# One input of four for a state-space scan computed on GpSimd instead of on VectorE, with its operands in SBUF

## What is computed

```
h = exp(dt_t[..., None] * A) * h + (dt_t * u_t)[..., None] * B_t[:, :, None, :]
y = jnp.einsum('bkdn,bkn->bkd', h, C_t)
```

## Time and profile before

| | |
|---|---|
| median of 3 runs | 13,516.15 us (13,488.19 to 13,520.65) |
| the profiled execution, its own time | 13,515.58 us |
| its span, first to last instruction | 13,513.4 us |
| VectorE busy | 11,024.0 us, 82% |
| TensorE matmul busy | 9,861.3 us, 73% |
| GpSimd busy | 8,026.4 us, 59% |
| ScalarE busy | 7,165.5 us, 53% |
| granted TensorE clock, mean | 0.701 of full speed |

### The profile page before, as it was taken

One profiled execution on the slowest core, in us unless ns is written; L12 is line 12 of the kernel. 1 busy time (PEld: TensorE's weight loads), 2 busy tenths in 40 slices (PEclk: granted clock), 3 DMA queues, 4 the chain that ended last, 5 costly groups with the idle time before them and its releaser, 6 DMA issues.

```text
span 13513.4 us, 97205 instructions
## 1 busy us (share of the span) xinstructions
PE 9861.3 (73%) x27968; PEld 2433.4 (18%) x27968; DVE 11024.0 (82%) x6747; ACT 7165.5 (53%) x10802; POOL 8026.4 (59%) x3463
## 2 busy tenths in 40 slices
PE   6866677766886677768777778776688667777665
PEld 1211112111221112212222112211122111221121
DVE  2999977998799988988789887899878998898700
ACT  3645545544465445666456654555446554576324
POOL 1667655666566766666666665566656776666500
PEclk8955577755786568769777777865679557776565
DMA  2655576555745555455564557655675555554410
GB/s 71 132 118 112 108 135 112 127 115 109 140 119 115 116 140 132 107 120 118 143 124 108 117 120 134 112 118 109 120 131 128 117 115 138 121 120 108 99 51 14
DMA packets 1742497, 1551.92 MB, mean 115 GB/s; under 512 B 1302398, under 2 KB 1303712, under 8 KB 1741964
## 3 DMA queue, kind: packets, MB, share of 16 engines
q1 hardware_dynamic: 1741964, 1545.71, 53.9%
HBM read 555.57 MB, written 184.55 MB: 55 GB/s over the span
## 4 chain that ended last, share of the span: by engine, by line
PE 27%; issue 26%; DVE 23%; ACT 8%; DMA 7%; POOL 4%; SPq 4%; DVEq 1%; POOLq 0%; ACTq 0%
DVE ps L1228 15%; DVE hs L1237 7%; PE ps L644 4%; PE ps L796 4%; DMA ust<-u_d 3%; PE ps L783 3%; PE ps L758 3%; PE ps L617 3%; POOL pr L1305 3%; PE ps L774 2%; ACT dec L1024 2%; PE ps L661 1%; DMA sd<-y_d 1%; SPq L528 1%; POOL sd L1273 1%
## 5 line engine op out<-in xcount | busy, mean ns | idle before, releaser
L1305 POOL TENSOR_TENSOR pr<-hs,crep 128x1024 f32<-128x1024 f32 x3072 | 7223.0, 2353 | 4490.9 <-DVE hs L1237 3209.6
L1237 DVE TENSOR_TENSOR_SCAN hs<-dec,carry,ps 128x1024 f32<-128x1024 f32 x2304 | 5406.4, 2347 | 303.6 <-ACT dec L1024 9.6
L1228 DVE TENSOR_TENSOR ps<-ps,dur 128x1024 f32<-128x1024 f32 x3072 | 3722.2, 1212 | 1038.3 <-PE ps L783 833.7
L783 PE MATMUL ps<-sbc,selb 96*128 96x512 bf16 x6144 | 2553.4, 510 | 2195.5 <-DVE hs L1237 2182.7
L1024 ACT ACTIVATE dec<-dtr,ac 128x1024 f32<-128x1024 f32 x3072 | 3489.8, 1137 | 981.8 <-DVE hs L1237 971.5
L796 PE MATMUL ps<-pr,red 128*32 128x512 f32 x12288 | 2387.8, 861 | 12.6 <-ACT yst L1039 7.0
L1031 ACT ACTIVATE carry<-hs 128x1 f32<-128x1 f32 x2304 | 460.2, 200 | 2758.7 <-DVE hs L1237 2755.7
L1237 DVE TENSOR_TENSOR_SCAN hs<-dec,zero,ps 128x1024 f32<-128x1024 f32 x768 | 1802.3, 2347 | 100.8 <-ACT dec L1024 2.9
L783 PEld LDWEIGHTS ps<-sbc,selb 96*128 96x128 bf16 x6144 | 510.0, 110 | 5057.2 <-DVE hs L1237 3847.0
L617 PE MATMUL ps<-xb,tapw 96*96 96x512 f32 x2304 | 1204.6, 635 | 21.0 <-ACT sd L871 18.5
L774 PE MATMUL ps<-xdf,tapw 6*96 6x512 f32 x1024 | 812.6, 884 | 166.1 <-ACT sbc L997 113.8
(11 more groups left out here) (113 smaller groups left out, 6108.7 us busy)
## 6 DMA issues: line engine op xcount, KB each, us to landing
dtr<-de SPq DMA_DIRECT2D x768, 512.0 KB, 7.6
dur<-us SPq DMA_DIRECT2D x768, 512.0 KB, 8.5
crep<-c_d SPq DMA_DIRECT2D x512, 512.0 KB, 6.9
ust<-u_d SPq DMA_DIRECT2D x256, 384.0 KB, 7.5
y_d<-yst SPq DMA_DIRECT2D x768, 128.0 KB, 3.7
sd<-y_d SPq DMA_DIRECT2D x512, 192.0 KB, 4.2
u_d<-sd SPq DMA_DIRECT2D x64, 384.0 KB, 3.1
z_d<-sd SPq DMA_DIRECT2D x64, 384.0 KB, 4.2
```

The costliest lines, as they stand in the source:

```text
L783: mm = pe.matmul(ps[:, SLOT + 2 * (n % RS) + hf, :], selb[:, i % GT // 2, :], sbc[:, w % 2, B * hf:B * (hf + 1)], start=True, stop=True)
L1228: dve.tensor_tensor(slot(n), slot(n), dur[:, 2 * (G % 2) + i % 2, :], ALU.mult).then_inc(bu_v, 1)
L1237: dve.tensor_tensor_scan(hs[:, n % RH, :], dec[:, n % RD, :], slot(n), init, ALU.mult, ALU.add).then_inc(scan_v, 1)
L1305: pool.tensor_tensor(pr[:, n % RP, :], hs[:, n % RH, :], crep[:, q, :], ALU.mult).then_inc(prod_g, 1)
```

## The change

For tiles 6 and 7 of each group (`on_pool`) TensorE makes no fill and VectorE no multiply. B of the last 4 states is spread by a DMA into a new SBUF buffer `brep`, and GpSimd multiplies `dur` by it in place. The scan of such a tile reads its decays and its input from SBUF. The other six tiles keep the PSUM path, and are renumbered by `others(n)` and `other(m)`, so that their slots, semaphore counts and look-ahead run over them alone: while tiles 6 and 7 are under way, the slots of the next group's first tiles can be filled.

With it go these: B is stored beside C (`bc_d`, 128 KB instead of 64 KB) and `load_b` is issued at tile 1; `load_u` is issued at tile 6 of step w for step w+2, where that belongs to the same sequence; `load_group` waits for the scans of the group whose room it takes, not for its multiplies; `yst` has one buffer instead of two, which makes room for `brep`.

```diff
+def on_pool(n):
+    return n % GT >= GT - 2
+def others(n):
+    return (GT - 2) * (n // GT) + min(n % GT, GT - 2)
+def other(m):
+    return GT * (m // (GT - 2)) + m % (GT - 2)
...
+            def load_b(w):
+                after(sp, bup_g, 2 * NG * w)
+                sp.wait_ge(c_out, 16 * (w + 1))
+                sp.dma_start(brep[:, :], bc_d[w % 2, NS - 4:NS, :].partition_broadcast(DB)).then_inc(brep_in, 16)
...
-                after(sp, bu_v, GT * (G - 1))
+                after(sp, scan_v, GT * (G - 1))
...
                     if i == 1:
+                        load_b(w)
                         load_c(NQ - 1, w)
-                        if w + 1 < W:
+                        if w + 1 < W and (w == 0 or (w + 1) % STEPS == 0):
                             load_u(w + 1)
+                    if i == 6 and w + 2 < W and (w + 2) % STEPS:
+                        load_u(w + 2)
...
-                after(pe, scan_v, n - RS + 1)
+                m = others(n)
+                after(pe, scan_v, other(m - RS) + 1 if m >= RS else 0)
...
-                    if n + 1 < W * NT:
-                        fill(n + 1)
+                    if not on_pool(n) and others(n) + 1 < W * NT * (GT - 2) // GT:
+                        fill(other(others(n) + 1))
...
-                after(act, y_out[E % 2], 32 * (E // 2))
+                after(act, y_out, 32 * E)
...
+                if on_pool(n):
+                    G = n // GT
+                    dve.wait_ge(bup_g, 2 * G + i % 2 + 1)
+                    dve.tensor_tensor_scan(hs[:, n % RH, :], dec[:, n % RD, :], dur[:, 2 * (G % 2) + i % 2, :], init,
+                                           ALU.mult, ALU.add).then_inc(scan_v, 1)
...
                 for i in range(NT):
-                    inp(w * NT + i)
+                    if not on_pool(i):
+                        inp(w * NT + i)
...
+            def input_on_pool(n):
+                w, G, j = n // NT, n // GT, n % 2
+                pool.wait_ge(bu_v, others(n - 2) + 1)
+                if n % NT == GT - 2:
+                    pool.wait_ge(brep_in, 16 * (w + 1))
+                v = dur[:, 2 * (G % 2) + j, :]
+                pool.tensor_tensor(v, v, brep[:, :], ALU.mult).then_inc(bup_g, 1)
...
                     product(w * NT + i)
+                    if i % GT in (3, 4):
+                        input_on_pool(w * NT + i + 3)
```

More of the change, by code:

```diff
@@ L141, in build_program @@
     t_d = dram("t_d", [nb, 2, CH, L])
-    c_d = dram("c_d", [2, NS, T])
+    bc_d = dram("bc_d", [2, 2 * NS, T])
     ctx = ExitStack()
@@ L168, in build_program @@
         crep = sb("crep", [128, NQ, T])
-        yst = sb("yst", [128, 2, B])
+        yst = sb("yst", [128, B])
+        brep = sb("brep", [128, T])
         carry = sb("carry", [128, NT])
@@ L284, in build_program @@
         ye_a = sem("ye_a")
-        y_out = [sem("y_out0"), sem("y_out1")]
+        y_out = sem("y_out")
+        brep_in, bup_g = sem("brep_in"), sem("bup_g")
         x_in = sem("x_in")
@@ L426, in post @@
                 cnt = done["post"]
-                for r in range(2):
-                    sp.wait_ge(y_out[r], 32 * (NG * STEPS // 2) * (j + 1))
+                sp.wait_ge(y_out, 32 * NG * STEPS * (j + 1))
                 after(sp, uz_out, 32 * C8 * done["pre"])
@@ L507, in store_c @@
                 sp.wait_ge(xd_a, 2 * w + 2)
-                sp.dma_start(c_d[w % 2], xdf[NS:2 * NS, :]).then_inc(c_out, 16)
+                sp.dma_start(bc_d[w % 2], xdf[0:2 * NS, :]).then_inc(c_out, 16)
             def load_c(q, w):
@@ L512, in load_c @@
                 sp.wait_ge(c_out, 16 * (w + 1))
-                sp.dma_start(crep[:, q, :], c_d[w % 2, 4 * q:4 * q + 4, :].partition_broadcast(DB)).then_inc(crep_in[q], 16)
+                sp.dma_start(crep[:, q, :], bc_d[w % 2, NS + 4 * q:NS + 4 * q + 4, :].partition_broadcast(DB)).then_inc(crep_in[q], 16)
+            def load_b(w):
+                after(sp, bup_g, 2 * NG * w)
+                sp.wait_ge(c_out, 16 * (w + 1))
+                sp.dma_start(brep[:, :], bc_d[w % 2, NS - 4:NS, :].partition_broadcast(DB)).then_inc(brep_in, 16)
             def load_group(g, w):
@@ L536, in store_y @@
                     sp.dma_start(y_d[s, k][2 * DB * g:2 * DB * (g + 1), t0:t0 + B],
-                                 yst[64 * hf:64 * (hf + 1), E % 2, :]).then_inc(y_out[E % 2], 16)
+                                 yst[64 * hf:64 * (hf + 1), :]).then_inc(y_out, 16)
             run(beside(plan[0], stages, False))
@@ L780, in fill @@
                     pe.wait_ge(s_a, 6 * w + 6)
-                after(pe, scan_v, n - RS + 1)
+                m = others(n)
+                after(pe, scan_v, other(m - RS) + 1 if m >= RS else 0)
                 for hf in range(2):
-                    mm = pe.matmul(ps[:, SLOT + 2 * (n % RS) + hf, :], selb[:, i % GT // 2, :],
+                    mm = pe.matmul(ps[:, SLOT + 2 * (m % RS) + hf, :], selb[:, i % GT // 2, :],
                                    sbc[:, w % 2, B * hf:B * (hf + 1)], start=True, stop=True)
@@ L995, in split @@
                 else:
-                    after(act, fill_p, NT * (w - 1))
+                    after(act, fill_p, others(NT * (w - 1)))
                 act.activation(sbc[:, w % 2, B * hf:B * (hf + 1)], ps[0:CH, PB, :], ACT.Identity).then_inc(s_a, 1)
@@ L1036, in collect @@
                 act.wait_ge(red_p, NP * w + NQ * (g + 1))
-                after(act, y_out[E % 2], 32 * (E // 2))
-                for dst, src in to_image(order[s][1], k, yst[:, E % 2, :], ps[:, YB, :]):
+                after(act, y_out, 32 * E)
+                for dst, src in to_image(order[s][1], k, yst[:, :], ps[:, YB, :]):
                     ins = act.activation(dst, src, ACT.Identity)
@@ L1226, in inp @@
                     dve.wait_ge(du_in[G % 2], 32 * (G // 2 + 1))
-                dve.wait_ge(fill_p, n + 1)
-                dve.tensor_tensor(slot(n), slot(n), dur[:, 2 * (G % 2) + i % 2, :], ALU.mult).then_inc(bu_v, 1)
+                dve.wait_ge(fill_p, others(n) + 1)
+                dve.tensor_tensor(slot(others(n)), slot(others(n)), dur[:, 2 * (G % 2) + i % 2, :], ALU.mult).then_inc(bu_v, 1)
             def states(n):
@@ L1234, in states @@
                 after(dve, carry_a, carries(n - RH + 1) if n >= RH else 0)
-                dve.wait_ge(bu_v, n + 1)
                 init = carry[:, i:i + 1] if w % NCH else zero[:, 0:1]
-                dve.tensor_tensor_scan(hs[:, n % RH, :], dec[:, n % RD, :], slot(n), init, ALU.mult, ALU.add).then_inc(scan_v, 1)
+                if on_pool(n):
[3 more added lines that the diff above has]
+                                           ALU.mult, ALU.add).then_inc(scan_v, 1)
+                else:
+                    dve.wait_ge(bu_v, others(n) + 1)
+                    dve.tensor_tensor_scan(hs[:, n % RH, :], dec[:, n % RD, :], slot(others(n)), init,
+                                           ALU.mult, ALU.add).then_inc(scan_v, 1)
             run(beside(plan[0], stages, False))
```

## The result

The changed kernel takes 14,045.85 us (median of 4 runs, 14,031.88 to 14,062.75) against 13,508.3 us of the kernel before, measured beside it: a ratio of 1.040, 95% interval 1.0381 to 1.0419. That is 538 us slower. The forecast was 13,815 us, in a range of 13,340 to 14,060: the sign and the mechanism were right, the size was not, since 300 us were forecast.

The account below looks back on a forecast made before the run. VectorE's chain was taken as the bound, 11,060 us plus some 1,455 of lateness from side work. The sum was 13,515.6 + 909 - 400 - 100 - 190 + 80 = 13,815 us, range 13,340 to 14,060.

Parts of the forecast that it names:

- The exclusion: A VectorE instruction with two SBUF inputs and a GpSimd instruction reading SBUF wait for each other; scans near 4.5 us.
- The quiet group: Eight tiles with hardly any side work: 1.7 us longer, the third group 3.7; a step 93.5 us, +909 us in all.
- the recovery: What takes up part of the 909 us: fill waits, early load, late groups, against dearer side work in `post`.
- (a): VectorE's waits for fills, 833.7 us, fall by missing fills and look-ahead: -400 us, bounds -208 and -650.
- (b): `load_u` issued a step earlier removes ScalarE's and TensorE's waits for it: -100 us, bounds 0 and -206.
- (c): Where a stall falls in tiles 4 or 5, scan 6 isn't held: 90 groups, -190 us, bounds 0 and -400.
- (d): GpSimd's multiply in `post` queues behind new inputs and blocked products while TensorE waits: +80 us, bound +290.
- Kept ports: Rival, chance 0.18: VectorE runs scans 6 and 7 in succession before product 5; a step 89.3 us, total 13,390 us.
- no exclusion for long scans: Rival, chance 0.06: long scans and GpSimd don't block each other; a step 78.4 us, total 12,500 to 12,700 us.
- waits merely change places: Rival, chance 0.03: either this or a larger recovery pays back the cost; total 13,516 us within 0.3%.
- GpSimd as the bound in `post`: Rival, chance 0.06: GpSimd also limits the steps with `post`, little is recovered and `load_b` is late; up to 14,506 us.
- costed at nothing: `load_b`, `load_c`, `dur` loads, one `yst` buffer and the larger store were expected to delay nothing; `load_b` uncovered would be +250 us.

Follow-up runs that it names:

- the two experiments above: Kernel before, VectorE's multiply of tiles 6 and 7 writing to SBUF: 14,242.19 us; changed kernel, decays of tiles 6 and 7 in PSUM, fill look-ahead dropped: 13,095.2 us.
- the late load: The changed kernel with the u values of step w+1 loaded at tile 1 of step w again: 14,314.35 us, ratio 1.0605.
- the last experiment: GpSimd's side work put ahead of each tile's product and input: changed kernel 14,040.09 us, with decays in PSUM 13,085.21, kernel before 13,510.48.

## Why the prediction was right, and what was mis-sized

**The exclusion** held, in both directions. The trace of before had shown it only on instructions of 1 and 96 elements, and it holds for scans of 1024. The Trainium skill (SBUF — State Buffer, § Who interferes with whom) states the rule for two-input instructions as such; the two experiments above, 3,334 ns with both inputs in SBUF and 2,326 with one in PSUM, agree.

**The quiet group** was sized right: 93.5 us for a step was forecast, 93.0 measured, and scans on `dur` near 4.5 us were 4,536 and 4,450 ns. First scans of two steps in a row, with no stall between them, in the kernel before and in the changed one:

```profile
1084.82 2.35 DVE L1237 TENSOR_TENSOR_SCAN hs<-dec,carry,ps 128x1024 f32<-128x1024 f32 x1
...
1171.32 2.35 DVE L1237 TENSOR_TENSOR_SCAN hs<-dec,carry,ps 128x1024 f32<-128x1024 f32 x1
```

```profile
4566.52 2.35 DVE L1269 TENSOR_TENSOR_SCAN hs<-dec,carry,ps 128x1024 f32<-128x1024 f32 x1
...
4659.46 2.35 DVE L1269 TENSOR_TENSOR_SCAN hs<-dec,zero,ps 128x1024 f32<-128x1024 f32 x1
```

A step went from 86.50 to 92.94 us, 6.44 more. Of 909 us on paper 128 x 6.44 = 824 came. In the third group the order was not the one worked out: scan 6 was to run right after product 4, and input 7 and product 5 went ahead of it. The two scans still ended 13.2 us after the start of scan 5, as forecast, because the same operations stand in a row in either order. That part of the size was right by this, not by the order.

**The step that failed is the recovery**, terms (a) to (d), -610 us. It came to 524 (the difference of the spans) - 824 = -300.

(b), forecast -100: the early load is worth -268 in the changed kernel, outside the bounds of 0 to -206. They were taken from its wait in the kernel before, and the change itself would have tripled that wait.

So (a), (c) and (d) together brought about -300 + 268 = -32 instead of -510 (the -268 is a difference between rounds, with its 15 us of doubt). VectorE's largest waits in the changed kernel:

```profile
DVE ps L1254 <- PE ps L809: 522.8, 219, 19.6
DVE sd L1186 <- ACT ps L929: 316.7, 50, 36.0
DVE xb L1191 <- PE ps L686: 262.5, 61, 7.8
```

(a): waits for fills fell by 311 us, from 833.7. But with the late load they are 706.1, so the change's own part, missing fills and look-ahead, is 128 us of it. Taken from the other side, with the early load in both kernels, it is 677.8 - 522.8 = 155. 400 had been forecast, and 208 was the low bound.

(c): all holds come to 1,640 us. VectorE's timeline in a quiet step gives this for the two scans together, of the first, the second and the third group:

```profile
4586.80 8.69 DVE L1265 TENSOR_TENSOR_SCAN hs<-dec,carry,dur 128x1024 f32<-128x1024 f32 x2
...
4617.03 8.69 DVE L1265 TENSOR_TENSOR_SCAN hs<-dec,carry,dur 128x1024 f32<-128x1024 f32 x2
...
4647.26 10.94 DVE L1265 TENSOR_TENSOR_SCAN hs<-dec,carry,dur 128x1024 f32<-128x1024 f32 x2
```

Unheld they would take 2.26 + 2.35 = 4.61. A quiet step holds its scans 2 x 4.08 + 6.33 = 14.5 us. That would be 1,855 us in 128 steps, so in all they were held about 215 us less. The trace bears the mechanism out: in 99 of the 384 groups the scan of tile 4 or 5 starts over 0.8 us late, and these groups are held 153 us less in all than the groups of the same place in the step without such a delay in tiles 3 to 5. (c), forecast as 90 groups and 190 us, was right in its mechanism and near in its size.

(d): VectorE's waits in the side work rose, by 70 us at L1186 (246.4 before) and 62 at L1191 (200.9 before), and 46 us for GpSimd's inputs are new. That is 178, not 80, and it isn't GpSimd's place in the queue.

Worked out of the waits, 824 - 311 - 215 + 178 = 476 us of the 524; some 48 us stay unassigned. What made the recovery small is therefore shown as an account, not as one cause: waits of VectorE that were taken away came back as others, and in the last experiment they did so one for one. Why that chain of side work keeps its length is open; it wasn't tried further.

**The rivals.** Kept ports is settled: product 5 goes ahead of scan 7 in the groups shown, and where VectorE was made to keep them, it paid only where GpSimd isn't behind. That there is no exclusion for long scans is refuted by their 4.5 us. The rival in which waits merely change places was priced at 13,516, the cost paid back; waits did change places, but the cost stayed. GpSimd as the bound in `post` did not come: those 4 steps took 17.2 us more, 4.3 each, less than the quiet ones; but (a) did stay under the low bound that this rival gave it. Of what was costed at nothing only `load_b` shows, and small: GpSimd waited 29.3 us in all for `brep`.

## What to carry to other kernels

Before moving an operand to SBUF, count the SBUF inputs of the VectorE instruction that will read it: here a second one made it and GpSimd's multiplies on SBUF wait for each other, and 768 such scans of 3,072 cost 5.5%. Where work is moved to GpSimd anyway, try leaving one input of its VectorE reader in PSUM: the same move then gained 3%, about half of it by the early load that came with it. Don't book a bottleneck's waits as a reserve that a new cost will use up: of 510 us booked, some 30 came. And price a transfer that is moved by its wait in the new queue, not in the old one.

## What the runs showed of the hardware

A held VectorE instruction doesn't always go first when GpSimd's running instruction ends. In the second group scan 6 went after one operation, with product 5 ready since about 4617.2 (an estimate, 2.42 us after the start of scan 5 as in the earlier trace rows); in the third it waited for the running one and was passed by two more, which followed each other 2.30 us apart (8.70 us in all). What decides is open: in both groups the scan had asked before GpSimd's next operation was recorded as started. The waiting time stands in the duration of the waiting instruction on both engines (VectorE 4.39 instead of 2.35 us, GpSimd 4.34 instead of 2.35), so a longer mean of an unchanged form of instruction is where to look for it.
